# Graph attention in one phase of four units, with the next unit prepared inside the loop of the current one

## The reference

```python
feat = jnp.einsum('nf,hfo->hno', x, W)
attn_self = jnp.einsum('hno,ho->hn', feat, a_self)
attn_neigh = jnp.einsum('hno,ho->hn', feat, a_neigh)
e = attn_self[:, :, None] + attn_neigh[:, None, :]
e = jax.nn.leaky_relu(e, 0.2)
e = e + MASK_VAL * (1.0 - adj)[None, :, :]
alpha = jax.nn.softmax(e, axis=-1)
out = jnp.einsum('hnm,hmo->hno', alpha, feat) + b[:, None, :]
return jax.nn.elu(jnp.transpose(out, (1, 0, 2)).reshape(out.shape[1], -1))
```

## Time and profile before

| | us |
|---|---|
| runs | 1440.71, 1444.09, 1448.41; median 1444.09 |
| the profiled execution, its own time | 1439.96 |
| its span in the trace | 1438.2 |
| PE busy (page, part 1) | 1167.0, 81% of the span |
| DVE busy | 820.2, 57% |
| ACT busy | 622.0, 43% |
| POOL busy | 225.7, 16% |
| mean granted PE clock | 0.886 of 2.4 GHz |

### The profile page before, as it was taken

One profiled execution on the slowest core, in us unless ns is written; L12 is line 12 of the kernel. 1 busy time (PEld: TensorE's weight loads), 2 busy tenths in 40 slices (PEclk: granted clock), 3 DMA queues, 4 the chain that ended last, 5 costly groups with the idle time before them and its releaser, 6 DMA issues. The chain is left out here.

```text
span 1438.2 us, 19822 instructions
## 1 busy us (share of the span) xinstructions
PE 1167.0 (81%) x7196; PEld 987.9 (69%) x7196; DVE 820.2 (57%) x2036; ACT 622.0 (43%) x1159; POOL 225.7 (16%) x252
## 2 busy tenths in 40 slices
PE   6959859869989899989699799725297998979888
PEld 3647647647957778878599689624175786858777
DVE  2366867667547465444476476455554655654544
ACT  3345846735526444434244144211063645623433
POOL 0000000004023032433000000000032403023332
PEclk9979968879979889989899999956599999979999
DMA  9200000000000022322000000000031000012222
GB/s 364 76 1 1 1 0 1 1 1 1 1 0 1 9 93 79 103 77 78 1 1 1 1 1 1 5 0 4 0 111 37 1 1 1 2 65 77 90 83 75
DMA packets 19280, 52.05 MB, mean 36 GB/s; under 512 B 3440, under 2 KB 5744, under 8 KB 19056
## 3 DMA queue, kind: packets, MB, share of 16 engines
q1 hardware_dynamic: 19184, 50.79, 10.9%
HBM read 49.73 MB, written 1.05 MB: 35 GB/s over the span
## 5 line engine op out<-in xcount | busy, mean ns | idle before, releaser
L1028 POOL TENSOR_TENSOR p_WML<-p_raw,p_WMH 128x768 fp32r<-128x768 f32 (+1 forms) x78 | 135.4, 1738 | 256.3 <-ACT p_WMH L1130 250.6
L203 PE MATMUL PS<-onesb,identb 128*128 128x512 bf16 x276 | 88.6, 465 | 50.6 <-PEq L163 36.8
L1188 ACT ACTIVATE p_AHI<-p_A 128x512 fp32r<-128x512 f32 x78 | 49.1, 629 | 177.4 <-DVE p_A L1329 177.3
L189 POOL TENSOR_SCALAR rstds<-mvs 128x4 f32<-128x4 f32 x16 | 3.7, 230 | 726.5 <-DVE mvs L184 249.7
L1329 DVE TENSOR_TENSOR p_A<-p_A,PS 128x512 f32<-128x512 f32 x62 | 42.6, 688 | 108.6 <-PE PS L1084 108.3
L1333 DVE TENSOR_TENSOR p_ALO<-p_A,p_AHI 128x512 fp32r<-128x512 f32 x78 | 61.9, 793 | 67.3 <-ACT p_AHI L1188 65.2
L80 PE MATMUL PS<-p_WMH,p_AHI 128*128 128x256 f32 x312 | 89.8, 288 | 12.8 <-DVE XS L1299 9.4
L802 PEld LDWEIGHTS PS<-p_V,p_PTS 128*128 128x128 f32 x768 | 94.8, 199 | 0.0
L802 PE MATMUL PS<-p_V,p_PTS 128*128 128x17 f32 x768 | 93.7, 262 | 0.0
L81 PE MATMUL PS<-p_WML,p_AHI 128*128 128x256 f32 x312 | 88.9, 285 | 0.0
L82 PE MATMUL PS<-p_WMH,p_ALO 128*128 128x256 f32 x312 | 88.8, 285 | 0.0
(11 more groups left out here) (353 smaller groups left out, 3329.7 us busy)
## 6 DMA issues: line engine op xcount, KB each, us to landing
p_raw<-in_moe SPq DMA_DIRECT2D x62, 448.0 KB, 3.2
p_fr<-in_fold SPq DMA_DIRECT2D x16, 512.0 KB, 7.9
p_raw<-in_ffn SPq DMA_DIRECT2D x16, 320.0 KB, 2.9
p_raw<-in_wpack SPq DMA_DIRECT2D x8, 416.0 KB, 8.4
CP<-in_consts SPq DMA_DIRECT2D x1, 1720.0 KB, 12.4
XS<-in_x SPq DMA_DIRECT2D x1, 1024.0 KB, 15.2
out<-XS SPq DMA_DIRECT2D x8, 128.0 KB, 2.5
p_ctr<-in_ctxT SPq DMA_DIRECT2D x1, 512.0 KB, 15.8
```

The costliest lines, as they stand in the source:

```text
L203: pe.matmul(PS[:, bank, :], identb[:, :], onesb[:, :].unsqueeze(1).broadcast_to([P, 4, P]), start=True, stop=True)
L1028: g.tensor_tensor(WML[:, n % RING, :], raw[:, n % RAW, 0:SEL], WMH[:, n % RING, 0:SEL].bitcast(F32), ALU.subtract).then_inc(s["w_lo"], 1)
```

## The change

The two phases become one, `graph_attention()`, over `UNITS` = (layer 0, half 0), (layer 0, half 1), (layer 1, half 0), (layer 1, half 1): 32 groups in one loop. Five things change.

1. What a unit needs is cut into jobs: `t` and `s` (the neighbour and self terms, 16 rows by 512 columns), `f0` and `f1` (`feat`, two tiles each), and for layer 1 `tr0` and `tr1` (transposes of the input). The jobs of unit u+1 are issued in the loop of unit u, one to a group, at steps 2 to 7 (`STEP`), into the spare bank 7. Each is PE's `job`, for all but `f` ACT's `high`, then DVE's `low`; a job waits for the `low` of the job before it.
2. The neighbour and self terms are summed by PE: a matmul of 64 rows gives s + t for two heads and 256 tokens (`scores`). Its right side `SR` is zero but for rows that SP fills with eight DMAs a unit, from `TB`, which holds the split `t`. POOL sets the constant rows in `setup`.
3. ACT applies the leaky ReLU as one `Prelu` of 1024 columns, PSUM to SBUF (`leaky`). ACT's four bias instructions and DVE's two of 512 columns go.
4. The bias moves into `feat`; the ELU is one exponential on ACT and two instructions on DVE. The output bank of the values is bank 6 alone.
5. All filler matmuls in the loops go; 24 are issued once, before the first group. The second half's mask is made by DVE during groups 0 to 3. In `setup` the ring of loads of `in_fold` shrinks from 8 to 5 buffers.

```diff
-                FR = 8
+                FR = 5
...
                     def _(g):
+                        g.wait_ge(s["xc_in"], 48)
+                        g.tensor_scalar(SL[:, :], const("onep").broadcast_to([P, TOK]), 1.0, None, ALU.mult).then_inc(s["r_set"], 1)
+                        for hd in range(GH):
+                            g.tensor_scalar(SR[:, hd, :], const("ohp")[:, hd:hd + 1].broadcast_to([P, TOK]), 1.0, None, ALU.mult).then_inc(s["r_set"], 1)
...
+                STEP = {"tr0": 2, "tr1": 3, "t": 4, "s": 5, "f0": 6, "f1": 7}
...
+                    def _(sp):
+                        for u in range(NU):
+                            sp.wait_ge(s["ax_v"], AT[u, "t"] + 1)
+                            if u >= 2:
+                                sp.wait_ge(s["z"], NG * (u - 1))
+                            for hd in range(GH):
+                                at = base(u) + 32 + hd
+                                sp.dma_start(SR[at:at + 9:8, hd, :].bitcast(F32), TB[hd:hd + 9:8, :].bitcast(F32)).then_inc(s["r_in"], 16)
...
+                        def scores(n):
...
+                            for q in range(2):
+                                hd = 4 * hg + 2 * q
+                                m = pe.matmul(PS[:, 2 * (n % 2) + q, :].rearrange("p (a k) -> p a k", a=2), SL[b:b + 64, t * P:t * P + P],
+                                              SR[b:b + 64, hd:hd + 2, (t // 2) * S:(t // 2) * S + S], start=True, stop=True)
+                            m.then_inc(s["z"], 1)
...
+                        for j in jobs(0):
+                            job(0, j)
+                        warm(pe, WARM["start"], bank=3)
+                        scores(0)
+                        scores(1)
+                        for n in range(NN):
+                            for u, j in due(n):
+                                job(u, j)
+                            if n:
+                                values(n - 1)
+                            if n + 2 < NN:
+                                scores(n + 2)
+                            weights(n)
+                        values(NN - 1)
...
+                        for n in range(NN):
+                            exps(n)
+                            if n + 2 < NN:
+                                leaky(n + 2)
+                            for u, j in due(n):
+                                if j[0] != "f":
+                                    high(u, j)
+                            weights(n)
+                            if n >= 2 and n % 2 == 0:
+                                elu((n - 2) // 2)
...
+                        for n in range(NN):
+                            if n + 1 < NN:
+                                shift(n + 1)
+                            v.wait_ge(s["pt"], 2 * n + 1)
+                            if n >= 2:
+                                v.wait_ge(s["pv"], n - 1)
+                            v.tensor_copy(PTS[:, n % 2, 0, :], PS[:, 4, :]).then_inc(s["pc_v"], 1)
+                            if n:
+                                outputs(n - 1)
+                            if n >= 3 and n % 2:
+                                elu((n - 3) // 2)
+                            for u, j in due(n):
+                                low(u, j)
+                            if n < TT:
+                                masks(1, n)
```

More of the change, by code:

```diff
@@ L72 @@
     "split": 8,
-    "weights": 4,
-    "elu": 4,
+    "start": 24,
 }
@@ L382, in _ @@
                         act.wait_ge(s["ext"], 12)
-                        act.activation(EH[:, :, :], ext[:, :, :], ACT.Copy).then_inc(s["ext_hi"], 1)
+                        for d in range(2):
+                            act.activation(EH[:, :, :].rearrange("p k (e d o) -> p k e d o", e=2, d=2)[:, :, :, d, :], ext[:, :, :, :], ACT.Copy).then_inc(s["ext_hi"], 1)
                         act.wait_ge(s["xc_in"], 48)
@@ L460, in _ @@
                     @block.gpsimd
                     def _(g):
-                        stats_gpsimd(g, s, h)
+                        for h in range(HALVES):
+                            stats_gpsimd(g, s, h, h)
                     @block.tensor
                     def _(pe):
-                        for l in range(2):
-                            kt = 1 if l == 0 else KC
-                            def left(k, lo, hi):
[L470 to L501, removed]
-                                for k in range(kt):
[L503 to L538, removed]
@@ new lines, in values @@
+                        def values(n):
+                            u, i = divmod(n, NG)
+                            t, hg = divmod(i, 2)
+                            pe.wait_ge(s["pc_v"], n + 1)
+                            pe.wait_ge(s["pc_a"], n + 1)
+                            pe.wait_ge(s["ax_v"], AT[u, "f1"] + 1)
+                            if n == 0:
+                                pe.wait_ge(s["ones"], 1)
+                            if n:
+                                pe.wait_ge(s["o_c"], n)
+                            for hh in range(4):
+                                for mt in range(2):
+                                    m = pe.matmul(PS[:, 6, hh * 33:hh * 33 + 33], PTS[:, n % 2, hh // 2, (hh % 2) * S + mt * P:(hh % 2) * S + mt * P + P],
+                                                  FT[:, u % 2, 2 * (t // 2) + mt, 4 * hg + hh, :], start=(mt == 0), stop=(mt == 1))
+                            m.then_inc(s["pv"], 1)
@@ new lines, in weights @@
+                        def weights(n):
+                            if n == 0:
+                                pe.wait_ge(s["ax_v"], AT[0, "s"] + 1)
+                            if n:
+                                pe.wait_ge(s["pc_v"], n)
+                                pe.wait_ge(s["pc_a"], n)
+                            for hh in range(4):
+                                pe.wait_ge(s["p"], 4 * n + hh + 1)
+                                for mt in range(2):
+                                    m = pe.transpose(PS[:, 4 + hh // 2, (hh % 2) * S + mt * P:(hh % 2) * S + mt * P + P],
+                                                     Z[:, n % 3, hh, mt * P:mt * P + P], ident)
+                                if hh % 2:
+                                    m.then_inc(s["pt"], 1)
@@ new lines, in high @@
+                        def high(u, j):
+                            l, h = UNITS[u]
+                            act.wait_ge(s["ax_pe"], AT[u, j] + 1)
+                            if j[0:2] == "tr":
+                                act.activation(HS[h][0][:, int(j[2]), :], PS[:, AUX, :], ACT.Copy).then_inc(s["ax_a"], 1)
+                            else:
+                                if his(AT[u, j]):
+                                    act.wait_ge(s["ax_v"], AT[u, j])
+                                act.activation(HI[0:16, :], PS[0:16, bank_of(u, j), :], ACT.Copy).then_inc(s["ax_a"], 1)
@@ new lines, in leaky, with exps @@
+                        def leaky(n):
+                            act.wait_ge(s["z"], n + 1)
+                            if n >= 3:
+                                act.wait_ge(s["pt"], 2 * (n - 2))
+                            act.activation(Z[:, n % 3].rearrange("p a k -> p (a k)"), PS[:, 2 * (n % 2):2 * (n % 2) + 2, :].rearrange("p a k -> p (a k)"),
+                                           ACT.Prelu, alpha=0.2).then_inc(s["pl"], 1)
+                        def exps(n):
+                            for hh in range(4):
+                                if hh % 2 == 0:
+                                    act.wait_ge(s["neg"], 2 * n + hh // 2 + 1)
+                                act.activation(Z[:, n % 3, hh, :], Z[:, n % 3, hh, :], ACT.Exp, bias=mx[:, n % 3, hh:hh + 1]).then_inc(s["p"], 1)
@@ new lines, in weights, with elu @@
+                        def weights(n):
+                            act.wait_ge(s["pt"], 2 * n + 2)
+                            if n >= 2:
+                                act.wait_ge(s["pv"], n - 1)
+                            act.activation(PTS[:, n % 2, 1, :], PS[:, 5, :], ACT.Copy).then_inc(s["pc_a"], 1)
+                        def elu(g):
+                            u, t = divmod(g, TT)
+                            act.wait_ge(s["o_c"], 2 * g + 2)
+                            if g >= 2:
+                                act.wait_ge(s["y"], g - 1)
+                            act.activation(EY[:, g % 2, :], XNS[:, TT * UNITS[u][1] + t, :], ACT.Exp).then_inc(s["y_e"], 1)
@@ new lines, in _ @@
+                        high(0, "t")
+                        high(0, "s")
+                        leaky(0)
+                        leaky(1)
+                        for n in range(NN):
[8 more added lines that the diff above has]
+                                elu((n - 2) // 2)
@@ L691, in small_attention @@
+                        outputs(NN - 1)
+                        elu(NN // 2 - 1)
         def small_attention(layer, h):
@@ L1820, in build @@
         setup()
-        for h in range(HALVES):
```

(6 more changed lines are left out.)

316 lines of the change are left out of this document (160 added, 156 removed).

## The result

The changed kernel takes 1492.31 us (median of four runs, 1485.99 to 1498.29) against 1444.8 for the kernel before on the same chip: ratio 1.033, 95% interval 1.027 to 1.039. It is slower. The prediction was 1429, faster by 11 us, with a range of 1396 to 1482: the sign came out the other way, and the measured time lies above the range. The profiled execution took 1486.61, 46.6 us more than the 1439.96 of before.

A forecast was written before the change was run, and what follows sets the result against it. No engine alone bounded the stage; 80 us lay outside its loops. Opening 97.1, base groups 128.7, jobs 35 and tail 7.2 gave 268; clock 33 made 301, 11 us less than before: 1429, range 1396 to 1482.

The forecast's parts named there:

- The opening: Stage start through unit 0's jobs, 24 fillers and first scores: group 0's first transposes end at 97.1 us.
- `setup`: Kernel's setup phase: POOL's nine added instructions and five load buffers instead of eight cost 0 us.
- Prelu: ACT's leaky ReLU of 1024 columns from PSUM in each group: 1.0 us, bounds 0.79 and 1.94.
- rival D: In the loop, Prelu and Exp need different tables; ACT reloads twice a group: 82 us, 1510 or more; chance 0.03.
- The ring: Base group's chain of scores, Prelu, ACT copy, handover, values: 4.15 us at full clock, 6.8 at half.
- The jobs: Groups with jobs for the next unit: PE's values wait behind jobs waiting for `low`; 35 us in all.
- The sum: Whole stage at 2.4 GHz: ends at 268.0 us against 312.3 before, 44 us less.
- the price of the clock: Loop, opening and tail at half clock: 96 us for 100%, 9.6 us per tenth of the loop at 1.2 GHz.
- the share of the loop at 1.2 GHz: New loop: a third at half clock, as in the loops before, adding 33 us; stage end 301.
- rival C: Loop from group 1 on: clock falls and hardly comes back; 1482 us at nine tenths, 1492 throughout; chance 0.32.
- the signs listed: Trace checks in the stage: transposes near 97, PE's waits, one table load, loop idle at most 2.5 us, clock 0.83.

The follow-up runs named there:

- the run with four fillers: Changed kernel with four filler matmuls of 512 columns put back into every group, between transposes and values: 1409.26 us, ratio 0.974 to the kernel before.
- the thin fillers: Changed kernel with four single-precision matmuls of 33 columns in each group, where another run had four of 512 columns: 1485.81 us, one run.

## Why the prediction was wrong

**The opening was right.** The first transposes of group 0 end at 94.98 + 1.91 = 96.9, given 97.1. Two parts offset each other: the jobs of unit 0 took 4.4 us on PE instead of 5.5, and from the scores to the end of the transposes it was 5.4 instead of 4.9. The eight DMAs and the rest fitted beside the 24 fillers. `setup` ends 0.2 us later, given 0: POOL's nine instructions and the ring of five are hidden. The loads of `in_fold` even land faster, 3.8 us in the median instead of 7.9.

**Prelu was right.** 1024 ns, given 1.0. ACT loads no table between 2 and 550 us, so rival D is out.

**The ring was 0.33 us short.** At full clock 4.48 us, given 4.15; the run with four fillers shows it on ACT:

```profile
187.24 1.03 ACT L620 ACTIVATE p_Z<-PS 128x1024 f32<-128x1024 f32 x1 [1.27 <-PE PS L552]
188.26 0.60 ACT L633 ACTIVATE p_PTS<-PS 128x512 f32<-128x512 f32 x1
...
191.72 1.02 ACT L620 ACTIVATE p_Z<-PS 128x1024 f32<-128x1024 f32 x1 [0.74 <-PE PS L552]
```

The values there start at 189.08. Copy 0.60 and 0.22 to the values, values 1.87, scores 0.77 to the next Prelu, Prelu 1.02: 4.48. Half of what was missing is the step from ACT's copy to PE, given 0.05; copy, values and scores took 0.05 to 0.07 more each than given. The members of the ring were right, and DVE does not close it: the values wait for ACT's copy. 31 groups make it 10 us. At half clock 7.38, given 6.8.

**The jobs were nearly right.** With four fillers and the clock at 0.95 the groups with jobs exceed the base group by 7.4 (unit 1), 11.9 and 14.0 us (units 2 and 3, starts of transposes 143.84 to 182.65 and 191.62 to 232.47, less 6 x 4.48): 33.3, given 35 for full clock. Each of the three holds a stretch at half clock, so at full clock it would be less. The kind of wait was right too. What I did not see is that the wait goes when the job is issued behind the values.

**The sum and the price of the clock came out, in part by luck.** Full clock throughout was to end the stage at 268. A clock of 0.95 is a tenth of the time at 1.2 GHz, by my price 9.6 us more: 278, and the run with fillers that the ring hides measured 278.6. But the ring was 10 us short, and what offset it is that the half-clock stretches lie mostly in groups with jobs, whose 33.3 us hold them already. With nine tenths at half clock the price gives 268 + 86 = 354; measured 354.5. That too is closer than its parts deserve: the ring was short at half clock as well, and which other parts were too high was not worked out.

**The step that failed is the share of the loop at 1.2 GHz.** "I take the third that the loops before had, no better and no worse": it was nine tenths, 53 us more. The term was carried over from loops that had 0.87 us of wide matmuls in each group of 3.99, to one whose only wide matmuls are the two of its scores, 0.66 us in each group of 4.48, and these did not hold the clock. The run without them shows what that assumption was worth: the loops before go from 0.81 and 0.87 to 0.50 and 0.56 without them. I had the row against it, the clock that fell at 181.8 after 16 values, and wrote that values do little to keep it up; and I had the argument, that at half clock the new ring has nothing to lift it. It stood under rival C with 0.32, and C came true: place, mechanism and size (nine tenths, 1482; measured 1486.6). What spoke for the third, the next phase's loop at 1.00 without fillers, had more wide matmuls in it, as I noted; and "the jobs are dense" held too little: the clock's two rises in the changed kernel are at jobs (119 and 280 us), but it fell again within 10 to 13 us, and when only their groups lacked fillers it stood at 0.50 just there.

Of the signs listed, wait for ACT's copy in base groups, wait for `low` in groups 4 to 7, the one table load and 96.9 came out; the clock (0.55, below the 0.7 that was named as C's mark) decided. In the trace PE was idle for up to 2.8 us before a job, a little above the 2.5 given.

That the clock, lost with the fillers, explains the loss in the stage is shown: one edit takes its end from 354.5 to 278.6, with the clock from 0.54 to 0.95, and the thin fillers at the same place do neither. The phases behind take 4 us more than before (46.6 less 42.2). Of these, 3.5 are time of PE on the same 5892 matmuls (929.2 us before, 932.7 after, 929.4 with four fillers). That points to the clock again; why it differs there stays open.

## What to carry to other kernels

Filler matmuls are a part of a loop's schedule: before removing them, ask of the new loop, group by group, what wide matmuls are left, and do not carry over the clock that the old loop had. Put them where PE waits for another engine anyway: here up to five cost a group nothing at full clock. And a step whose input is made on another engine belongs behind the work on PE that others wait for, not ahead of it.

## What the runs showed of the hardware

PE occupied without a break is not PE at full clock. In the run with thin fillers it was busy for 46.00 of 46.00 us, for 5.1 us of each 8.0 us group with matmuls of 33 columns and their weight loads, at a granted clock of 0.50. The same place filled for about as long (1.56 us with the thin ones, 1.70 with the wide, at half clock) with 512 columns of BF16 or of single precision gives a stage clock of 0.95 and 0.93. In the changed kernel the granted clock stayed at its lower level for 144 us in a row with PE 86% busy.

A matmul of 64 rows and 512 columns takes as long as one of 128 rows. Four in a row span 1.21 us at full clock with 64 rows (L552, from 91.47 in the changed kernel) and 1.20 with 128 (L479, from 144.68 in the kernel before). But two of 64 rows in the loop take 0.66 us from their start to the start of the transposes behind them (104.45 to 105.11, in the run with four fillers), 0.16 more than two at the rate of a row, and 1.15 at half clock. The weight load of the first transpose starts there together with its matmul, at 105.11, where in the kernel before the load of the transposes starts at 116.62 and their first matmul at 116.83. Why it comes late was not tried.
